# Reordering the front, the attention seam and the layer seam of a two-layer graph-attention kernel

## The chip, the cores and the metric

The kernel runs on one core of one Trainium2 chip. The metric is the device time of one execution in microseconds. All engines of the core (TensorE, VectorE, ScalarE, GpSimd, SyncE) run their own instruction queues in order and meet at semaphores.

## The reference

x has 3327 rows of 256, adj is a 0/1 matrix of 3327 x 3327. Two blocks follow one another, each ahead of a layer norm with relu and with a residual. Cut to what matters:

```
h = relu(layernorm(x))
# block 0: graph attention (both adjacencies are adj)
hs = h @ W_sa ; g = h @ W_gcnb
e = where(adj, exp(-leaky(s_left + s_right)), 0)   # s_left, s_right = hs @ a_sa
x_a = (e @ hs) / (rowsum(e) + 1e-5) ; x_b = adj @ g + b
x = x + sigmoid(gate_a * x_a + gate_b * x_b)        # gates: sigmoid of adj @ h and h against Wa, Wb
# block 1: two layers
y = relu(layernorm(x))
for W in W_stack:                                    # 256 x 512
    Wh, Ws = split(y @ W)
    a = softmax(Wh @ Ws.T) * adj
    y = leaky_relu(a @ Wh + y)
out = x + y
```

## The kernel before, in words

Rows are cut into 26 tiles of 128, 13 pairs of 256 rows (PAIRS) and 13 units of 256 columns (UNITS). Every product is made in three passes of a high and a low part (`product3`, line 1349: 6 matmuls for 256 rows deep), so each operand is evicted from PSUM twice: a high part by ScalarE (ACT) and the remainder, the low part, by VectorE (DVE).

**Front** (the loops `for p in range(PAIRS)`, lines 652, 1033, 1432, and 513 on GpSimd (POOL)). For each pair of tiles: layer norm (`statistics`, `variances`, on POOL the power `inverse_root`, `scales`, `normalise`), a transpose of the pair on TensorE (PE) (`transpose0`), evicted by `transposed_high` and `transposed_low`, the products G (`products_g`, `g_high`, `g_low`) and H (`products_h`, `h2_high`, `h2_low`, which also copies the scores s_right, s_left). From pair 2 on PE takes one unit of block 0's attention (`unit0`, lines 1422 to 1426, 20 matmuls) after each pair; its operand is made by `leaky0`, `exp0` (ACT), `mask0` (DVE), `high0` (ACT), `low0` (DVE). Transposes, G and H share four banks of PSUM in a ring; `turn(pr, i)` numbers the uses (i = 0 the transpose, 1 and 2 G, 3 and 4 H), `projected(i)` waits for the low part of the use four turns before. Before the change the transpose of pair p+1 is at the head of iteration p. Then come 169 units of `unit0` in all, N_LATE says up to which unit leaky, high and exp stand in that order. Adjacency comes by POOL's DMA queue, six stages ahead (`load_unit`).

**Block 1.** Projections `project_wh(n)` (n 0 to 12 layer 1, 13 to 25 layer 2) and `project_q(b)`, then an order written out by hand in steps v. In step v PE makes the scores of unit g (`scores`, S_AT) and weighs the unit 16 steps older (`weigh`, A_AT; after unit CH = 169 four steps more, GAP). Between them a unit goes: `maximum` (DVE), `evict` (ACT, line 706), `subtract` (POOL, 534), `exponent` (ACT, 718), `mask` (DVE, 1158) and `total` (DVE, 1168), `high` (ACT, 752), `low` (POOL, 541), `weigh` (PE, 1562 to 1565). Scores use banks 0 and 1, exponents banks 2 and 3, sums over a block 4 and 5, Q and the turned maximum 6, turned sums 7. A block b is 13 units. At its end of scores (S_END) the maximum is turned (`turn_max`, `row_max`, `spread_max`, `turn_max_back`, `keep_max`); at its end of weighing (A_END) the sum (`turn_sum`, `row_sum`), and the reciprocal comes back in one of two ways: for a block in NEAR by `spread_rec`, `turn_sum_back` and `keep_rec`, for the others by DMA (`store_rec`, `load_rec`, R_END three steps later). Then `weighted`, `residual` twice, `leaky`, `x2_high`, `x2_low`; x2 of blocks 0 to 11 is stored and loaded back by SP (`store_x2`, `load_x2`), block 12's goes straight to XT. The layer's W is split into high and low parts at step v = 154 (lines 872, 1318, 1320).

**Layer seam** (WH_AT): steps 181 to 187 hold projections 13 to 25, with the weighing of layer 1's last units to step LAST1 = 184 and layer 2's scores of block 13 going on. Their banks and waits before the change:

```
334 def wh_bank(n):
338     return 5 if u < 4 else 2 + u % 2
716 if g == CH: act.wait_ge(wh_lo, LAYERS * UNITS)
1507 pe.wait_ge(x2_d, PAIRS - 1); pe.wait_ge(wh_lo, n)          # u < 4
1510 pe.wait_ge(sum_d, CH); pe.wait_ge(wh_lo, n - 1)            # u >= 4
```

The last block (LB = 25) is weighed with rows as outputs (`row_exponent`, line 728, `turn_last`, line 1576, `weigh_last`).

## Time and profile before

| what | value |
|---|---|
| median of 3 runs | 1569.0 us (1568.11 to 1570.0) |
| the profiled execution's own time | 1568.53 us |
| its span | 1566.7 us |
| PE busy | 1533.8 us, 98% |
| DVE, ACT, POOL busy | 1130.7, 1068.2, 983.9 us |
| front with the first attention units | 0 to about 89 us |
| block 0's attention to | about 484 us |
| layer seam | about 1030 to 1070 us |

Times of rows are microseconds from the span's start. A timeline row gives start, busy time, engine, line, operation, output and input, count, and in brackets how long the engine sat idle before it and what ended that. Rows on one engine follow one another a little closer than their busy times, since the end of one overlaps the start of the next. A wait for several semaphores is put down to the one that came last.

### The profile page before, as it was taken

To read this page: it belongs to the slowest core of one execution; us is meant where nothing else is said; L and a number is where in the kernel's file an instruction comes from. 1 tells how busy PE (TensorE), PEld (TensorE's weight loads), DVE (VectorE), ACT (ScalarE), POOL (GpSimd) and SP (SyncE) were. 2 spreads that over 40 slices of the span, in tenths; PEclk is the share of its full clock that TensorE was granted. 3 is DMA by queue.
4 is the path that set the end of the run, shared out by engine and by line. 5 is a ranking of instruction groups with operands and counts; after the bars stand their busy time and mean duration, and the time that the engine had idled before them with its cause. 6 is when DMAs were issued, how large, how long until landed. Compare 5 with 4: busy or idle time off the path is not lost.

```text
span 1566.7 us, 34636 instructions
## 1 busy us (share of the span) xinstructions
PE 1533.8 (98%) x12826; PEld 1524.1 (97%) x12826; DVE 1130.7 (72%) x2119; ACT 1068.2 (68%) x2081; POOL 983.9 (63%) x886
## 2 busy tenths in 40 slices
PE   6999999999999999999999999999999999999998
PEld 5999999999999999999999999999999999999997
DVE  7667666676675677777777777766777777777774
ACT  5689899899984566666666666646666666666666
POOL 4312222222210488888888888847888888888885
PEclk9999999999999999999999999999999999999999
DMA  4354444544440134343433435522443333334343
GB/s 162 65 101 122 116 119 117 149 117 120 116 101 28 42 92 106 107 109 99 107 107 107 111 105 174 183 62 81 104 105 104 104 105 105 104 105 105 105 108 106
DMA packets 98423, 167.83 MB, mean 107 GB/s; under 512 B 15951, under 2 KB 28878, under 8 KB 97998
## 3 DMA queue, kind: packets, MB, share of 16 engines
q1 hardware_dynamic: 70208, 117.75, 27.3%
q0 software_dynamic: 24336, 44.31, 12.0%
q10 hardware_dynamic: 3710, 3.56, 0.7%
q8 instruction: 101, 1.65, 0.5%
q14 instruction: 68, 0.56, 0.1%
HBM read 152.44 MB, written 13.14 MB: 106 GB/s over the span
## 4 chain that ended last, share of the span: by engine, by line
PE 88%; issue 4%; DVE 3%; DMA 2%; POOL 2%; ACT 1%; SPq 0%; DVEq 0%; POOLq 0%; ACTq 0%
PE PS L1349 32%; PE PS L1562 9%; PE PS L1565 9%; PE PS L1564 9%; PE PS L1426 5%; PE PS L1423 5%; PE PS L1425 5%; PE PS L1424 5%; PE PS L1422 5%; POOL FR L541 1%; DMA STGT<-adjt 1%; DMA ROW<-rec_scratch 1%; DMA rec_scratch<-COL 1%; POOL X L534 1%; DVE AF L1158 0%
## 5 line engine op out<-in xcount | busy, mean ns | idle before, releaser
L541 POOL TENSOR_TENSOR FR<-AF,FR 128x512 fp32r<-128x512 f32 x338 | 451.3, 1335 | 124.4 <-ACT FR L752 118.6
L1349 PE MATMUL PS<-FR,RB 128*128 128x256 f32 x3900 | 513.9, 281 | 1.8 <-ACT X L706 1.7
L1349 PEld LDWEIGHTS PS<-FR,RB 128*128 128x128 f32 x3900 | 481.7, 188 | 3.1 <-ACT X L706 3.0
L534 POOL TENSOR_TENSOR X<-X,ROW 128x512 f32<-128x512 f32 x283 | 369.2, 1305 | 81.9 <-ACT ROW L762 81.9
L1562 PE MATMUL PS<-FR,RA 128*128 128x256 f32 x1300 | 370.7, 285 | 3.2 <-POOL FR L541 3.2
L1565 PE MATMUL PS<-FR,RA 128*128 128x256 f32 x1300 | 365.0, 281 | 0.0
L1564 PE MATMUL PS<-FR,RA 128*128 128x256 f32 x1300 | 364.4, 280 | 0.0
L481 POOL DMA_DIRECT2D STGT<-adjt x169 | 91.3, 540 | 298.0 <-PE PS L1426 295.9
L1158 DVE TENSOR_TENSOR AF<-PS,AJ 128x512 f32<-128x512 f32 x338 | 231.1, 684 | 56.1 <-ACT PS L718 46.1
L706 ACT ACTIVATE X<-PS 128x512 f32<-128x512 f32 x272 | 162.5, 597 | 158.8 <-DVE AF L1090 151.4
L1090 DVE TENSOR_TENSOR AF<-PS,AF 128x512 f32<-128x512 f32 x286 | 196.4, 687 | 101.0 <-PE PS L1349 98.6
L1562 PEld LDWEIGHTS PS<-FR,RA 128*128 128x128 f32 x1300 | 244.9, 188 | 5.6 <-POOL FR L541 3.9
L1564 PEld LDWEIGHTS PS<-FR,RA 128*128 128x128 f32 x1300 | 245.1, 189 | 0.0
L1565 PEld LDWEIGHTS PS<-FR,RA 128*128 128x128 f32 x1300 | 244.9, 188 | 0.0
L752 ACT ACTIVATE FR<-AF 128x512 fp32r<-128x512 f32 x338 | 214.0, 633 | 44.6 <-DVE AF L1158 40.4
L718 ACT ACTIVATE PS<-X 128x512 f32<-128x512 f32 x283 | 167.9, 593 | 56.5 <-POOL X L534 54.9
L1168 DVE TENSOR_TENSOR AF<-PS,AF 128x512 f32<-128x512 f32 x300 | 203.8, 679 | 0.0
L1422 PE MATMUL PS<-RA,FR 128*128 128x258 f32 x676 | 191.5, 283 | 3.1 <-DVE FR L967 3.1
L1426 PE MATMUL PS<-RB,STGT 128*128 128x258 f32 x676 | 192.2, 284 | 0.0
L1423 PE MATMUL PS<-RA,FR 128*128 128x256 f32 x676 | 191.5, 283 | 0.0
L1425 PE MATMUL PS<-RB,STGT 128*128 128x258 f32 x676 | 191.3, 283 | 0.0
L1424 PE MATMUL PS<-RA,FR 128*128 128x258 f32 x676 | 190.4, 282 | 0.0
(175 smaller groups left out, 2408.1 us busy)
## 6 DMA issues: line engine op xcount, KB each, us to landing
AJ<-adjt SPq DMA_DIRECT2D x338, 256.0 KB, 2.7
STGT<-adjt POOLq DMA_DIRECT2D x169, 256.0 KB, 3.0
xt_scratch<-ROW SPq DMA_DIRECT2D x12, 512.0 KB, 2.6
RB<-xt_scratch SPq DMA_DIRECT2D x12, 512.0 KB, 5.3
x_scratch<-X ACTq DMA_DIRECT2D x13, 256.0 KB, 2.2
ROW<-x_scratch SPq DMA_DIRECT2D x13, 256.0 KB, 3.2
out<-ROW SPq DMA_DIRECT2D x12, 256.0 KB, 3.4
ROW<-rec_scratch SPq DMA_DIRECT2D x22, 128.0 KB, 3.8
```

Source lines behind the costliest of these rows:

```text
L534: nc.gpsimd.tensor_tensor(slot, slot, MB.unsqueeze(1).broadcast_to([P, 2, 256]), ALU.subtract)\
L541: nc.gpsimd.tensor_tensor(LO[g % 2], WA[g % 2], HI[g % 3].bitcast(F32), ALU.subtract)\
L1158: nc.vector.tensor_tensor(WA[g % 2], PS[:, 2 + g % 2, :], ADJ[g % NADJ], ALU.mult).then_inc(mask_d, 1)
L1349: last = nc.tensor.matmul(out, stationary(a, k), moving(b, k), start=(k == 0 and i == 0), stop=(k == K - 1 and i == 2))
L1422: nc.tensor.matmul(e_to[:, 0:GX], e_hi, RA[:, j, 0:GX], start=first, stop=False)
L1423: nc.tensor.matmul(e_to[:, 0:D], e_hi, RA[:, j, GX:GX + D], start=False, stop=False)
L1424: nc.tensor.matmul(e_to[:, 0:GX], e_lo, RA[:, j, 0:GX], start=False, stop=final)
L1425: nc.tensor.matmul(a_to[:, 0:GX], adj, G[:, j, 0:GX], start=first, stop=False)
L1426: last = nc.tensor.matmul(a_to[:, 0:GX], adj, G[:, j, GX:2 * GX], start=False, stop=final)
L1562: nc.tensor.matmul(to, w_hi_, hi, start=(u == 0 and h == 0 and d == 0), stop=False, skip_group_check=True)
L1564: nc.tensor.matmul(to, w_hi_, lo, start=False, stop=False, skip_group_check=True)
L1565: last = nc.tensor.matmul(to, w_lo_, hi, start=False, stop=final, skip_group_check=True)
```

## The change

In the front the transpose of pair p+1 goes between G and H of pair p, on PE, ACT and DVE, with a new numbering of turns; DVE takes the first low part ahead of the variances, the mask ahead of G's low parts, `scales` of a chain at the end of the same pair; POOL's power goes ahead of the load. In block 1 project_wh(2) goes ahead of project_q(0), xt_low(12) one step later; W's split goes to steps 159 and 160. Block 11 leaves NEAR (reciprocal by DMA) but keeps x2 on chip; block 24's reciprocal comes two steps later. In the layer seam the projections use banks 5, 0, 1, 2, 3, evictions (EV_AT) have steps of their own, block 13's maximum is turned before the scores. The diff, cut:

```
-N_LATE = UNITS + 1
+N_LATE = 2 * UNITS + 1
+EV_AT = dict(WH_AT)
+EV_AT |= {182: (13,), 183: (14,), 184: (15, 16, 17, 18, 19, 20), 185: (21,), 186: (22,), 187: (23, 24), 188: (25,)}
+WH2_BANK = (5, 0, 1, 5, 0, 1, 2, 3, 5, 2, 3, 5, 2)
 WH_AT |= {181: (13,), 182: (14,), 183: (15,), 184: (16, 17, 18, 19, 20, 21), 185: (22,), 186: (23, 24), 187: (25,)}
+W2_AT = 159
-NEAR = (PAIRS - 2, PAIRS - 1, LB - 1)
+NEAR = (PAIRS - 1, LB - 1)
+FAR_X2 = PAIRS - 2
-R_END = {v + 3 * (b not in NEAR): b for v, b in A_END.items()}
+R_END = {v + (0 if b == PAIRS - 1 else 2 if b == LB - 1 else 3): b for v, b in A_END.items()}
...
-            return 5 if u < 4 else 2 + u % 2
+            return WH2_BANK[u]
         def turn(pr, i):
-            return 5 * pr + i + 1 if i else max(5 * pr - 4, 0)
+            return 5 * pr + (0, 1, 2, 4, 5)[i] if i else max(5 * pr - 2, 0)
         def bank_of(pr, i):
-            return 0 if turn(pr, i) == 1 else 4 + turn(pr, i) % 4
+            return 4 + turn(pr, i) % 4
...
@@ SP, load_x1 and steps @@
-                    sp.wait_ge(x2_st, 16 * (PAIRS - 1))
+                    sp.wait_ge(x2_st, 16 * FAR_X2)
...
-                if b is not None and b < PAIRS - 1:
+                if b is not None and b < FAR_X2:
                     store_x2(b)
-                for u in range(PAIRS - 1):
+                for u in range(FAR_X2):
@@ POOL @@
-            normalise(2)
-            for p in range(1, PAIRS - 2):
-                if p - 1 in LN_CHAIN:
-                    i = LN_CHAIN[p - 1]
-                    inverse_root(i, *LN_PARTS[i])
-                normalise(p + 2)
+            for p in range(PAIRS - 2):
+                normalise(p + 2)
+                if p in LN_CHAIN:
+                    i = LN_CHAIN[p]
+                    inverse_root(i, *LN_PARTS[i])
@@ ACT front @@
             for p in range(PAIRS):
-                if 1 <= p < PAIRS - 1:
-                    transposed_high(p + 1)
...
                 g_high(p, 0)
+                if p == PAIRS - 1:
+                    high0(p - 1)
                 g_high(p, 1)
-                if p == 0:
-                    transposed_high(1)
-                if p >= 2:
-                    high0(p - 1)
+                if p < PAIRS - 1:
+                    transposed_high(p + 1)
...
+                if 2 <= p < PAIRS - 1:
+                    high0(p - 1)
                 h2_high(p, 0)
@@ ACT exponent @@
-                if g == CH:
-                    act.wait_ge(wh_lo, LAYERS * UNITS)
+                if CH <= g < CH + 2:
+                    act.wait_ge(wh_lo, UNITS + 1 + max(m for m in range(UNITS) if WH2_BANK[m] == 2 + g % 2))
@@ ACT x2_high @@
-                if b == PAIRS - 1:
+                if b >= FAR_X2:
+                    act.wait_ge(s_mm, CH)
@@ ACT before and in the steps @@
+            wh_high(2)
             q_high(0)
             post_store(PAIRS - 1)
-            wh_high(2)
...
-                if A_END.get(v - 1) in NEAR and v - 1 != LAST1:
-                    keep_rec(A_END[v - 1])
-                if x is not None and x < GL:
+                if x is not None and x < GL and x != CH:
                     exponent(x)
                 if e is not None:
                     evict(e)
+                if x == CH:
+                    exponent(x)
...
+                if A_END.get(v - 2) == LB - 1:
+                    keep_rec(LB - 1)
-                if v == a_step(GL) + 2:
+                if v == a_step(GL) + 3:
                     keep_rows()
...
-                for i, n in enumerate(WH_AT.get(v, ())):
+                for i, n in enumerate(EV_AT.get(v, ())):
+                    if v == LAST1 and i == 1:
+                        spread_rec(A_END[v])
                     wh_high(n)
-                    if v == LAST1 and i == 0:
+                    if v == LAST1 and i == 1:
                         keep_rec(A_END[v])
-                    if v == LAST1 and i == 2:
+                    if v == LAST1 and i == 3:
                         x2_high(A_END[v])
@@ DVE front @@
-            dve.wait_ge(x_in[1], 16)
-            statistics(2, 4)
             dve.wait_ge(wg_hi, 1)
...
             dve.wait_ge(x_in[1], 16)
+            statistics(2, 4)
             statistics(4, 6)
+            transposed_low(0)
             variances(1, 2, 6, 3)
-            transposed_low(0)
             scales(1, 2, 6)
...
             for p in range(PAIRS):
-                if 1 <= p < PAIRS - 1:
-                    transposed_low(p + 1)
-                g_low(p, 0)
-                if p - 1 in LN_CHAIN:
-                    i = LN_CHAIN[p - 1]
-                    scales(i, *LN_PARTS[i])
                 if p >= 2:
                     mask0(p - 1)
+                g_low(p, 0)
                 g_low(p, 1)
-                if p == 0:
-                    transposed_low(1)
+                if p < PAIRS - 1:
+                    transposed_low(p + 1)
...
+                if p in LN_CHAIN:
+                    i = LN_CHAIN[p]
+                    variances(i, *LN_PARTS[i], 3 + sum(b <= LN_PARTS[i][1] for a, b in LN_STATS.values()))
                 if p == 1:
                     mask0(0)
+                if p == PAIRS - 1:
+                    low0(p - 1)
                 h2_low(p, 0)
-                if p >= 1:
+                if 1 <= p < PAIRS - 1:
                     low0(p - 1)
                 h2_low(p, 1)
                 if p in LN_CHAIN:
                     i = LN_CHAIN[p]
-                    variances(i, *LN_PARTS[i], 3 + sum(b <= LN_PARTS[i][1] for a, b in LN_STATS.values()))
+                    scales(i, *LN_PARTS[i])
@@ DVE steps @@
+            wh_low(2)
             q_low(0)
             post_norm(PAIRS - 1)
-            wh_low(2)
...
-                if v == 154:
-                    dve.wait_ge(w_hi, 4)
+                if v == W2_AT:
+                    dve.wait_ge(w_hi, 3)
...
+                if v == W2_AT + 1:
+                    dve.wait_ge(w_hi, 4)
...
-                if v == X12_AT:
+                if v == X12_AT + 1:
                     xt_low(PAIRS - 1)
@@ PE front @@
             for p in range(PAIRS):
-                if 1 <= p < PAIRS - 1:
-                    transpose0(p + 1)
                 pe.wait_ge(htlo_done, p + 1)
                 products_g(p)
-                if p == 0:
-                    transpose0(1)
-                    pe.wait_ge(w_ready, 1)
                 if p == 1:
                     turn_left()
+                if p < PAIRS - 1:
+                    transpose0(p + 1)
+                if p == 0:
+                    pe.wait_ge(w_ready, 1)
                 products_h(p)
@@ PE project_wh @@
-                elif u < 4:
+                elif wh_bank(n) in WH2_BANK[:u]:
+                    pe.wait_ge(wh_lo, UNITS + 1 + max(m for m in range(u) if WH2_BANK[m] == WH2_BANK[u]))
+                else:
                     pe.wait_ge(x2_d, PAIRS - 1)
-                    pe.wait_ge(wh_lo, n)
-                else:
-                    pe.wait_ge(sum_d, CH)
-                    pe.wait_ge(wh_lo, n - 1)
+                    if wh_bank(n) < 2:
+                        pe.wait_ge(ev_d, SEAM)
+                    elif wh_bank(n) < 4:
+                        pe.wait_ge(sum_d, CH)
@@ PE scores @@
+                if SEAM <= g < SEAM + 2:
+                    pe.wait_ge(wh_lo, UNITS + 1 + max(m for m in range(UNITS) if WH2_BANK[m] == g % 2))
...
-                if b == PAIRS and u == UNITS - 1:
-                    pe.wait_ge(x2_d, PAIRS)
+                if b == PAIRS and u >= FAR_X2:
+                    pe.wait_ge(x2_d, u + 1)
@@ PE steps @@
+            project_wh(2)
             project_q(0)
-            for n in range(2, 6):
+            for n in range(3, 6):
...
+                if S_END.get(v - 1) == PAIRS:
+                    turn_max(PAIRS)
                 if s is not None:
                     scores(s)
...
                 for i, n in enumerate(WH_AT.get(v, ())):
+                    if i == 0 and S_END.get(v - 1) == PAIRS:
+                        turn_max_back(PAIRS)
                     project_wh(n)
```

## Rows read from the trace of the kernel before

**Rows 1.** The page, part 4: the chain that ended last, by engine.

```profile
PE 88%; issue 4%; DVE 3%; DMA 2%; POOL 2%; ACT 1%; SPq 0%; DVEq 0%; POOLq 0%; ACTq 0%
```

**Rows 2.** Windows: length, busy us (x instructions) PE, PEld, DVE, ACT, POOL; clock, DMA share, GB/s.

```profile
8.60:35.00 26.40, 20.00 (x141) 19.00 (x142) 21.99 (x80) 16.25 (x41) 13.70 (x18) 1.00 0.44 151
945.00:960.00 15.00, 14.61 (x121) 14.14 (x120) 11.53 (x19) 9.28 (x18) 11.40 (x10) 1.00 0.26 73
999.50:1018.00 18.50, 18.04 (x151) 17.63 (x151) 15.39 (x27) 11.95 (x23) 16.10 (x13) 1.00 0.41 123
1030.60:1070.40 39.80, 35.64 (x286) 34.03 (x286) 22.59 (x39) 17.85 (x34) 11.45 (x10) 1.00 0.11 30
1150.00:1500.00 350.00, 350.00 (x2972) 350.00 (x2971) 267.38 (x455) 214.97 (x383) 297.98 (x232) 1.00 0.39 105
1528.00:1543.00 15.00, 12.54 (x102) 11.55 (x102) 10.86 (x21) 11.45 (x34) 8.83 (x7) 1.00 0.33 93
```

**Rows 3.** Timeline of DVE: start, us, engine, line, form, count [idle before <-releaser].

```profile
8.77 0.68 DVE L1022 TENSOR_TENSOR WX<-AJ,WX 128x516 fp32r<-128x516 f32 x1
...
10.15 0.38 DVE L902 BATCH_NORM_AGGREGATE MV<-ROW 128x2 f32<-128x6 f32 x4
...
11.47 0.68 DVE L934 SCALAR_TENSOR_TENSOR FR<-PS,FR 128x512 fp32r<-128x512 f32 x1
...
13.47 0.79 DVE L928 TENSOR_SCALAR AF<-X,LNT 128x256 f32<-128x256 f32 x2
```

**Rows 4.** Timeline of PE in the front.

```profile
12.29 2.92 PE L1349 MATMUL PS<-WX,FR 128*128 128x258 f32 x12 [3.79 <-DVE FR L934]
15.01 1.06 PE L1376 MATMUL PS<-IDN,AF 128*128 128x128 f32 x4
...
58.34 0.28 PE L1422 MATMUL PS<-RA,FR 128*128 128x258 f32 x1
```

**Rows 5.** Timeline of DVE and ACT over one pair of the front.

```profile
38.40 0.15 DVE L952 COPY XS<-PS 128x4 f32<-128x4 f32 x1
...
39.59 0.63 ACT L596 ACTIVATE AF<-AF 128x512 f32<-128x512 f32 x1
...
40.87 0.68 DVE L961 TENSOR_TENSOR AF<-AF,STGT 128x512 f32<-128x512 f32 x1
...
41.80 1.39 DVE L894 BATCH_NORM_STATS2 ROW<-X 128x6 f32<-128x256 f32 x4
...
44.11 0.15 DVE L952 COPY XS<-PS 128x4 f32<-128x4 f32 x1
```

**Rows 6.** Timeline of PE and DVE at the start of the second attention.

```profile
487.62 1.67 PE L1349 MATMUL PS<-RB,WX 128*128 128x256 f32 x12 [1.28 <-DVE RB L1065]
...
493.34 0.68 DVE L1072 TENSOR_TENSOR RA<-PS,RA 128x512 fp32r<-128x512 f32 x1
...
508.81 1.68 PE L1349 MATMUL PS<-FR,RB 128*128 128x256 f32 x12 [0.61 <-ACT X L706]
```

**Rows 7.** Timeline of DVE, the second subtraction of W.

```profile
949.64 1.78 DVE L1320 TENSOR_TENSOR WX<-ROW,WX 128x512 fp32r<-128x512 f32 x1
```

**Rows 8.** Timeline of DVE, weighting of block 10.

```profile
972.49 0.70 DVE L1197 TENSOR_TENSOR PS<-PS,ROW 128x512 f32<-128x512 f32 x1 [1.71 <-DMA ROW<-rec_scratch]
```

**Rows 9.** Timeline of PE and ACT in the layer seam.

```profile
1037.69 0.39 PE L1562 MATMUL PS<-FR,RA 128*128 128x256 f32 x1 [0.87 <-POOL FR L541]
...
1049.50 3.06 PE L1349 MATMUL PS<-WX,RB 128*128 128x256 f32 x24 [0.28 <-DVE RA L1072]
...
1065.45 0.60 ACT L718 ACTIVATE PS<-X 128x512 f32<-128x512 f32 x1 [0.84 <-DVE RA L1072]
...
1068.96 0.36 PE L1562 MATMUL PS<-FR,RA 128*128 128x256 f32 x1 [0.66 <-POOL FR L541]
```

**Rows 10.** Timeline of DVE and PE in the tail.

```profile
1536.43 0.70 DVE L1197 TENSOR_TENSOR PS<-PS,ROW 128x512 f32<-128x512 f32 x1 [2.46 <-ACT ROW L771]
...
1539.42 0.66 PE L1576 MATMUL PS<-IDN,PEB 128*128 128x128 f32 x4 [1.65 <-ACT PEB L728]
```

More of the change, by code:

```diff
@@ L864, in _ @@
                     spread_max(S_END[v - 1])
-                if A_END.get(v) in NEAR:
+                if A_END.get(v) in NEAR and v != LAST1:
                     spread_rec(A_END[v])
@@ L1356, in projected @@
                     return
-                i -= 8 if i - 4 == turn(PAIRS, 0) else 4
+                i -= 4
                 if i == 0:
@@ L1361, in projected @@
                     q, j = (i - 1) // 5, (i - 1) % 5
-                    if j == 0 and q == 0:
-                        return
-                    if j == 0:
+                    if j == 2:
                         pe.wait_ge(htlo_done, q + 2)
-                    elif j < 3:
-                        pe.wait_ge(glo_done, 2 * q + j)
+                    elif j < 2:
+                        pe.wait_ge(glo_done, 2 * q + j + 1)
                     else:
@@ L1489, in project_q @@
                     pe.wait_ge(wx_ready, 5)
-                if b >= PAIRS and i < PAIRS - 1:
+                if b >= PAIRS and i < FAR_X2:
                     pe.wait_ge(xt2_in[i % 4], 16 * (i // 4 + 1))
@@ L1552, in weigh @@
                 if b == PAIRS:
-                    pe.wait_ge(wh_lo, UNITS + max(4, u + 1))
+                    pe.wait_ge(wh_lo, UNITS + max(1 + max(m for m in range(UNITS) if WH2_BANK[m] == 4 + b % 2), u + 1))
                 pe.wait_ge(alo_d, g + 1)
@@ L1694, in _ @@
                 for i, n in enumerate(WH_AT.get(v, ())):
+                    if i == 0 and S_END.get(v - 1) == PAIRS:
+                        turn_max_back(PAIRS)
                     project_wh(n)
-                    if i == 0 and S_END.get(v - 1) is not None:
+                    if i == 0 and S_END.get(v - 1) not in (None, PAIRS):
                         turn_max_back(S_END[v - 1])
```

17 lines of the change are left out of this document (9 added, 8 removed).

## Prediction

> **What bounds the kernel now.** I read the page first, then the stretches where TensorE (PE) does not keep its pace, then the order of events in each. On the page 88% of the chain that ended last runs over PE [rows 1]. So the time is PE's work plus PE's holes, and the change neither adds nor removes a product of weight: it takes out two small transposes and moves the rest. What is to be had is holes only. The windows show their size [rows 2]. In the undisturbed 1150 to 1500 us, 2972 matmuls take 350 us, 0.118 us each, and nothing is lost; twelve (one unit of scores, one of weighting, one projection) are 1.41 us. At that price 8.6 to 35 us holds 141 matmuls or 16.6 us of work in 26.4 us; 945 to 960 loses 0.7; 999.5 to 1018 loses 0.7; the seam between the two layers (1030.6 to 1070.4) has 286 or 33.7 in 39.8, so 6.1 lost; the tail 1528 to 1543 has 102 or 12.0 in 15, so 3.0 lost. Single waits stand in the timeline. A few matmul records may be missing, so the losses are upper bounds.
>
> **Front, start.** Today the low part of the first transpose stands behind the statistics, the aggregates and the variance adds. It starts at 11.47 [rows 3] and the first products at 12.29 [rows 4]. In the change it takes the place of the aggregates (10.15), and the subtraction at 8.77 moves ahead of the wait on x; so about 9.5, and products at 10.35: 1.9 us earlier. But the second transpose needs normalise(1), at 13.47 on VectorE (DVE), which hangs on the power on GpSimd (POOL) and does not move. Its two operations take 0.79; so the transpose starts at 14.35 instead of 15.01. 0.7 is left, and H waits for the same.
>
> The first twelve products took 2.92 us [rows 4], 0.24 each against 0.118 later, while the granted clock reads 1.00 in the window row. That pace is the lower of the two levels (1.2 GHz), after four transposes and 3.79 us without work. The change leaves a hole of about 1.2 us before the second transpose. Were H and G behind it at the low level too, 24 products would take 2.9 us more. I charge nothing, because the next wait (the turn of the left scores, bound by DVE at 19 to 20 us) covers about half of it and the DVE loop below the rest. The Trainium skill (TensorE: Matmul & The Clock Gate, Part 1: The HAM clock gate) says the half-rate clock follows idleness; by it the new hole would speak against this part.
>
> **Front, per pair.** One pair's loop today: the copy of the right scores (38.40), exp (39.59), mask (40.87), statistics (41.80), next copy (44.11) [rows 5]: 5.7 us. PE has 24 products, 4 transposes and 20 unit matmuls per pair, the same 5.7 us. The transposed low part (0.6) hides today in DVE's wait for G's high part. In the change mask comes first (exp starts 1.19 after the copy, 0.65 more to its end and hand-over: 1.85), then two G low parts (0.34 each), the transposed low part 0.6, statistics 1.31, H low 0.40, unit low 0.60. With the mask's 0.60 that is 6.0 us while statistics last (pairs up to 4), 4.7 after. And the new order of PSUM turns makes H(p,1) wait for G's low part of the same pair, behind that mask; T(p+1) now waits for H's low part of the pair before. Walking pair by pair with today's start-to-start times I find the gain of the start gone by pair 2, whose unit products begin 0.8 late, those of pair 4 0.9 late, and those of pair 7 at 58.8 against 58.34 [rows 4]: **0.5 lost**. After pair 5 the low part of G is ready 1.3 us after G begins and H(p,1) asks for it at 2.5 less the hand-over, 2.1: it holds, 5.7 again. Bounds: 3 gained (the start's 1.9 and two of today's waits) to 4 lost. The power goes ahead of one load of adjacency on POOL's queue, 1.7 us later for a stage wanted six units on: nothing. The stall near 101 us on a load behind the strided store of scores keeps its place, both issue in the same order. N_LATE only keeps leaky, high, exp in the old order for 13 more units, 2.0 us of ScalarE (ACT) work per unit of 2.4: nothing.
>
> **Start of the second attention.** PE waits 1.28 us for the last transposed low part before project_q(0) [rows 6]; project_wh(2) now stands there. But project_wh(5) needs wh_low(3), which stays behind post_scales at 493.34; so it starts at about 493.8 instead of 494.1 and most of the hoist becomes a later hole. With one refill less, **0.4** (0 to 1.3). The wait of 0.61 at 508.81 exists because xt_low(12) stands ahead of maximum(6); it moves behind it: **0.7** with the refill (0.3 to 0.8).
>
> **W of layer two.** Two subtractions with both inputs in SBUF sit in one step; the second takes 1.78 us and ends at 951.4 [rows 7], right before the turn of a block's maximum, for which PE waits: the 0.7 lost in that window. They go to steps 159 and 160. There DVE has 1.0 us free per step (three operations of 0.6 in 2.82), but block 10's residual work (five of 0.6) follows from step 162. **0.4** (0.6 lost to 0.9 gained).
>
> **Block 11 by DMA.** The two transposes back go (128 columns each, about 0.06, and a refill), and x2's store and load; the reciprocal goes by store and broadcast, three steps later. Today PE loses 0.7 there [rows 2] besides; the far block 10 loses too, its weighting waits 1.71 us for that DMA [rows 8]. **0.3** (1.0 lost to 1.2 gained). SP's queue gets a small store and a 128 KB broadcast ahead of one adjacency load, and loses 1 MB.
>
> **Layer seam.** Today a projection's high and low parts stand in the same step ahead of the next exponent: PE waits 0.87 at 1037.69. Projections share bank 5 or two banks, so each waits for a forerunner's low part (0.28 and a refill at 1049.50). Then come block 13's maximum and an eviction, and weigh(169) waits 0.66 for low(169) at 1068.96, because exponent(169), at 1065.45, waits for all 26 low parts [rows 9]. With five banks no projection waits: each bank's last reader is two or more projections back, 2.8 us, against 1.3 for high and low. Evictions are a step late, so exponents 167 and 168 go first; turn_max goes before the scores and its back turn before wh(23). By hand: wh(13..15) at 1032.1, 1034.9, 1037.8; wh(16..21) 1040.9 to 1049.8 (block 12's x2 done at 1048.5, in time for scores(181)); scores(184) end at 1061.8; exponent(169) starts at 1060.4 and takes 3.5 us through mask, high and POOL's low, as today from 1065.45 to 1068.96, so weigh(169) starts at 1063.9 after a hole of 0.7. exponent(170) waits for wh_low(25): 0.3 more. So 5.1 less 0.3, **4.8** (2 to 6.1).
>
> **Tail.** Block 24's reciprocal comes two steps later. Today DVE's weighted(24) waits 2.46 us, to 1536.43, ahead of a mask; its high part and an exponent follow, for whose transpose PE waits 1.65 us [rows 10]. Moved, mask(326) needs only its own transpose; the wait goes. weighted(24) then delays mask(328), 0.2 back. **1.5** (0 to 2.1).
>
> **Sum.** -0.5 + 0.4 + 0.7 + 0.4 + 0.3 + 4.8 + 1.5 = 7.6 us off the profiled execution's 1568.5: 1560.9. The median of the runs is 1569.0, 0.5 above it; I forecast 1561.2 us for it. A measurement of this kernel can tell about 0.2% (3.1 us) from no change.
>
> **Rivals.** (1) The front is worth more: if ACT and DVE run ahead where I have them wait, the start's 1.9 lives: 2.5 us less, 1558.7. For: PE has 9.8 us of holes before 35. Against: the 6.0 us loop. 0.15. (2) The seam gives half: exponents 169 and 170 still wait for low parts of projections 23 and 25 behind ACT's queue; 2.4 in place of 4.8, with the tail at 0.5: 1564.6. For: the 3.5 us chain behind the exponent is untouched. 0.14. (3) DVE and POOL shut each other out: both moved subtractions take 1.78, not one, and block 10's work queues behind them, 1.0 us of stall: W's term -0.6, 1562.2. For: one already took 1.78 while POOL, 85% busy in steady state (297.98 of 350 us), ran. 0.10. The skill's page SBUF — State Buffer (Who interferes with whom) states it as a rule: such a DVE operation and a GpSimd operation block one another for a whole instruction; the trace agrees. (4) Slower: H(p,1)'s new wait on G's low part binds in every pair after 5 too. It decides once the low part comes over 2.1 us after G begins, where I find 1.3; the whole is slower only if ten pairs lose over 0.8 us each. At 1.4 each, 14 less the 8.1 of the other terms is 6 on top: 1575. For: all of DVE's front work is now in that chain. 0.04. (5) The holes reappear behind POOL's 2.6 us per step, and nothing that can be measured is left: 1567 to 1569. 0.05.
>
> **From this to the numbers.** The main case has 0.52, with 1558.5 to 1564. Case 1 reaches 1557, case 2 1566. The range of 1557 to 1566.5 leaves out cases 4 and 5 and the edges of the others. Faster by over 0.2% means under 1565.9: the main case, cases 1 and 3 and three quarters of case 2, 0.87. Same 0.09, slower 0.04.
>
> **What would show it.** First products at about 10.3 us, unit products of pair 7 at 58.3 to 59.3. No PE wait before project_q(0), one near 493; none on ACT at 508. From projection 13 to weigh(169) 31.8 us where today has 36.9, with no wait on a projection's low part before scores(184). The 1.65 us of the tail gone. I am wrong if PE's holes before 89 us shrink or grow by over 2, or if the seam gives under 3.

## The result, and the profile after

The kernel after takes **1559.0 us** (median of 4 runs, 1557.3 to 1559.3) against 1568.55 us for the kernel before on the same chip (4 runs, 1568.0 to 1570.0): a ratio of 0.9941, 95% interval 0.9929 to 0.9953. That is 9.6 us faster. The forecast was 1561.2 us, from 1557 to 1566.5. The profiled execution took 1559.26 us with a span of 1557.5 us, so 9.3 us less than the profiled one of before.

The page first. The chain that ended last now runs over PE for 91% where it was 88% [rows 1]; the work on PE is the same, so what went is holes:

```profile
PE 91%; issue 2%; DVE 2%; DMA 2%; POOL 1%; ACT 1%; POOLq 0%; SPq 0%; DVEq 0%; ACTq 0%
```

Then the same stretches as in [rows 2], each moved to where that work now lies (columns as there: length, busy us and instructions of PE, PEld, DVE, ACT and POOL, clock, DMA share, GB/s):

```profile
8.60:35.00 26.40, 20.34 (x128) 19.08 (x128) 21.29 (x82) 15.99 (x42) 14.19 (x20) 1.00 0.44 148
942.50:957.50 15.00, 15.00 (x130) 15.00 (x129) 10.28 (x19) 9.58 (x18) 12.13 (x11) 1.00 0.27 74
998.10:1015.40 17.30, 17.30 (x151) 17.30 (x150) 14.61 (x25) 10.87 (x19) 16.05 (x13) 1.00 0.48 105
1028.00:1062.80 34.80, 34.31 (x291) 34.13 (x290) 22.49 (x39) 17.49 (x34) 11.21 (x10) 1.00 0.11 31
1150.00:1500.00 350.00, 350.00 (x2973) 350.00 (x2972) 266.66 (x453) 216.10 (x384) 298.66 (x232) 1.00 0.41 105
1520.30:1535.30 15.00, 13.99 (x115) 13.03 (x114) 10.81 (x21) 12.01 (x36) 9.05 (x7) 1.00 0.37 107
```

Three things stand out. The two windows around layer two's W and block 11 are full, 15.00 of 15 and 17.30 of 17.3 us. The seam's work fills 34.31 of 34.8 us, where 35.64 of 39.8 was busy before. And the front has not gained: 128 matmuls in 26.4 us where 141 were before, in the same stretch; its holes are as large as ever. The steady stretch is the same to one instruction (2973 and 2972), so nothing comes from there.

**Where the 9.3 us lie.** I laid the two timelines of PE over one another by their order of instructions and read after minus before at the same instruction: -0.1 at the first full unit of the front (unit 15, 102 us); +0.2 at 496; -0.4 at 510; -0.4 at 700; -1.5 at 800; -2.4 at 960; -1.3 at 982; -2.6 at 1015; -7.6 at 1065; -7.7 at 1520; -9.2 at 1553. The code between 541 and 940 us is the same in both kernels, so the 1.1 us between 700 and 800 belongs to those two executions and not to the change (the traces of e7, e8, e9 and e10, with that same code, have steps of 0.3 to 0.7 us there too), and so may other steps of that size. That is why each part was then undone by itself.

The rows that answer to the forecast's. PE in the front and at the start of the second attention (timeline: start, us, engine, line, form, count, idle before and its releaser), for [rows 4] and [rows 6]:

```profile
10.36 2.92 PE L1361 MATMUL PS<-WX,FR 128*128 128x258 f32 x12 [1.89 <-DVE FR L945]
13.92 1.11 PE L1386 MATMUL PS<-IDN,AF 128*128 128x128 f32 x4 [0.64 <-DVE AF L939]
14.69 5.25 PE L1361 MATMUL PS<-WX,FR 128*128 128x260 f32 x24
...
28.10 0.99 PE L1361 MATMUL PS<-WX,FR 128*128 128x260 f32 x6 [1.41 <-DVE RB L953]
...
59.47 0.28 PE L1432 MATMUL PS<-RA,FR 128*128 128x258 f32 x1
...
102.39 0.39 PE L1432 MATMUL PS<-RA,FR 128*128 128x258 f32 x1 [1.28 <-DVE FR L978]
...
494.40 1.65 PE L1361 MATMUL PS<-WX,RB 128*128 128x256 f32 x12 [2.03 <-DVE RA L1082]
```

The first products start at 10.36, as forecast (10.35). At 14.69, 24 products take 5.25 us, 0.22 each: by their pace still the lower level (1.2 GHz) that the first twelve had, although the column of the granted clock reads 1.00 there. At 28.10 is the new wait of H(2,1) for the low part of its own pair's G. Pair 7's unit products start at 59.47, 1.13 us later than before. The wait ahead of project_q(0) is gone and one of 2.03 stands ahead of project_wh(5).

DVE around block 10's residual work, for [rows 7] and [rows 8]:

```profile
962.33 1.74 DVE L1328 TENSOR_TENSOR WX<-ROW,WX 128x512 fp32r<-128x512 f32 x1 [0.62 <-ACT WX L880]
966.49 1.37 DVE L1332 TENSOR_TENSOR WX<-ROW,WX 128x512 fp32r<-128x512 f32 x1 [0.62 <-ACT WX L882]
971.20 0.70 DVE L1207 TENSOR_TENSOR PS<-PS,ROW 128x512 f32<-128x512 f32 x1 [0.95 <-DMA ROW<-rec_scratch]
```

PE in the seam, for [rows 9]:

```profile
1039.80 7.37 PE L1361 MATMUL PS<-WX,RB 128*128 128x256 f32 x60
...
1060.87 0.35 PE L1576 MATMUL PS<-FR,RA 128*128 128x256 f32 x1 [0.49 <-POOL FR L546]
...
1064.20 0.36 PE L1576 MATMUL PS<-FR,RA 128*128 128x256 f32 x1 [0.28 <-POOL FR L546]
```

Five projections run in one piece, and from projection 13 (1029.49) to weigh(169) (1060.87) it is 31.38 us: 36.90 before, 31.8 forecast.

### The profile page after: what moved, and what is told of

Its sections match the earlier page's. It is cut to its first block, busy times and chain, and to the rows that moved or that the text cites. A ratio compares the mean times of both kernels' runs of the same rounds, so it can differ in the third digit from the quotient of the medians.

```text
span 1557.5 us, 34619 instructions
## 1 busy us (share of the span) xinstructions
PE 1531.8 (98%) x12824; PEld 1524.5 (98%) x12824; DVE 1132.0 (73%) x2119; ACT 1068.5 (69%) x2079; POOL 982.1 (63%) x886
## 3 DMA queue, kind: packets, MB, share of 16 engines
q8 instruction: 101, 1.65, 0.5%
## 4 chain that ended last, share of the span: by engine, by line
PE 91%; issue 2%; DVE 2%; DMA 2%; POOL 1%; ACT 1%; POOLq 0%; SPq 0%; DVEq 0%; ACTq 0%
PE PS L1361 34%; PE PS L1576 9%; PE PS L1579 9%; PE PS L1578 9%; PE PS L1436 5%; PE PS L1433 5%; PE PS L1435 5%; PE PS L1432 5%; PE PS L1434 5%; POOL FR L546 1%; DMA STGT<-adjt 1%; DMA ROW<-rec_scratch 0%; POOL X L539 0%; DMA X<-xt 0%; DVE ROW L905 0%
## 5 line engine op out<-in xcount | busy, mean ns | idle before, releaser
L972 DVE TENSOR_TENSOR AF<-AF,STGT 128x512 f32<-128x512 f32 x169 | 116.8, 691 | 111.3 <-ACT AF L601 100.0
L1432 PE MATMUL PS<-RA,FR 128*128 128x258 f32 x676 | 191.6, 283 | 2.3 <-DVE FR L978 2.2
```

The source lines that it names most:

```text
L1432: nc.tensor.matmul(e_to[:, 0:GX], e_hi, RA[:, j, 0:GX], start=first, stop=False)
```

## The experiments

Each is the kernel after with one edit (e7: two, e12: three); the edits are shown cut. A profile's place can be read to 0.1 us, but two executions of one code differ by about 1 us, so with each result stands what its trace shows at the place of the edit. Ratios are to the kernel before on the same chip; several of these chips ran all kernels 0.5 to 3 us slower or faster than the first.

**e1, the seam.**

```
-WH2_BANK = (5, 0, 1, 5, 0, 1, 2, 3, 5, 2, 3, 5, 2)
+return 5 if u < 4 else 2 + u % 2
-EV_AT |= {182: (13,), 183: (14,), 184: (15, ..., 20), ...}
+EV_AT = WH_AT
+(turn of maximum behind the scores)
```

> The kernel after, with the seam of the kernel before alone: all projections of layer two in bank 5 or in banks 2 and 3, their high and low parts in their own step, the turn of block 13's maximum behind the scores. My theory (the seam's order is the term of 4.8 us, and the two profiles put 5.0 there): 1559.0 + 5.0 = 1564.0 us; from projection 13 to weigh(169) 36.5 to 37 us in place of 31.4; the waits 0.87 at exponent 168's place and 0.66 ahead of weigh(169) are back. Rival (the seam gains half only, and the rest of the fall behind projection 13 is block 11's x2 that needs no store and load any more): 1561.5, from projection 13 to weigh(169) 34 us. Rival (the profiles differ by chance elsewhere and the seam is worth all of the fall): over 1565.

Measured: 1564.16 us (10 runs), ratio 0.9976 (0.9967 to 0.9985). The three other kernels of that chip keep the new seam: 1558.23 (e2), 1559.28 (e3) and 1560.30 us (e4). PE:

```profile
1028.75 1.60 PE L1353 MATMUL PS<-WX,RB 128*128 128x256 f32 x12
...
1065.63 0.36 PE L1563 MATMUL PS<-FR,RA 128*128 128x256 f32 x1 [0.65 <-POOL FR L542]
```

36.88 us, with the old waits. Against after it loses 5.5 us up to weigh(169), and 4.97 us once weigh(170) is through, since after waits 0.28 there and a little behind. The seam's order is worth 5.0, forecast 4.8. My theory stands, both rivals fall.

**e11, the turn of the maximum alone.**

```
-if S_END.get(v - 1) == PAIRS: turn_max(PAIRS)      (ahead of the scores)
+if S_END.get(v - 1) is not None: turn_max(...)      (behind them; the back turn behind project_wh)
```

> The kernel after, with only the turn of block 13's maximum back behind the scores and behind the first projection of its step; banks and evictions of the seam as in after. Theory A (the banks carry the seam's gain, the turn's place little): 0 to 0.7 us slower, 1559.0 to 1559.7, from projection 13 to weigh(169) 31.4 to 32.1. Rival B (the kernel with the whole old seam waited 0.84 us for that maximum's turn and 1.14 us for an eviction behind it, and both belong to the turn's place): 2.0 us slower, 33.4.

Measured: 1559.97 us, ratio 0.9933 (0.9918 to 0.9947). 31.90 us from projection 13 to weigh(169), whose wait grows from 0.49 to 0.99; 0.5 there and 0.2 behind. Theory A: banks and eviction times carry 4.3, the turn's place 0.7.

**e2, the front as before; e3, the old pair loop with the new start and the new last pair.**

> The kernel after, with the front of the kernel before alone (transposes ahead of the products of G, turns, low part of the first transpose behind the variances, power behind, last pair's unit products in their old place). The two profiles: the products of G of the last pair start 1.07 us later in after, unit 15 of the front 0.09 us earlier. Theory A (the loss of the pairs is given back at the last pair and at the wait for a load of adjacency near 101 us): first products at 12.3 in place of 10.36 us, G of the last pair at 83.8, unit 15 at 102.4 to 102.6, time 1559.1, within 0.4 of after. Rival B (my forecast's term, 0.5 lost, is still there at the end): 1558.5. Rival C (the start's 1.9 us lives on in part): 1560 or more.

> The kernel after, with the pair loop and the turns of the kernel before, but the new start (low part of the first transpose ahead of the variances) and the new place of the unit's parts in the last pair. Theory A (what sets the end of the front is the load of adjacency behind the strided store of the scores, near 101 us): first products at 10.4, G of the last pair at 83.6 to 84.0, and yet unit 15 at 102.2 to 102.5 with a wait of 2 us or more ahead of it; time 1558.6 to 1559.2. Rival B (the new pair loop costs its 1.07 us to the end): unit 15 at 101.3, time 1557.9. Rival C (the start's gain is not eaten up by the old loop either): unit 15 at 100.5 or before, 1557.0.

Measured: e2 1558.23 us, ratio 0.9943 (0.9928 to 0.9958); e3 1559.28 us, 0.9947 (0.9930 to 0.9963). Neither can be told from after. The traces tell why, for e3 (first DVE, then PE):

```profile
101.58 0.69 DVE L977 TENSOR_TENSOR AF<-AF,STGT 128x512 f32<-128x512 f32 x1 [4.09 <-DMA STGT<-adjt]
...
93.82 0.36 PE L1441 MATMUL PS<-RA,FR 128*128 128x258 f32 x1 [2.40 <-DVE FR L983]
102.93 0.39 PE L1441 MATMUL PS<-RA,FR 128*128 128x258 f32 x1 [0.19 <-DVE FR L983]
```

In e3 the last pair's products of G start 1.6 us before those of after (83.25 and 84.84), and two things take that back. The first is the chain on ACT and DVE behind the last pair. Its start, the copy of the last right scores on DVE, did not move with PE (DVE, first of after, then of e3):

```profile
88.34 0.23 DVE L963 COPY XS<-PS 128x4 f32<-128x4 f32 x2 [0.21 <-ACT RA L581]
88.56 0.22 DVE L968 COPY XS<-PS 128x4 f32<-128x4 f32 x2
```

In before it stands at 88.40 and in e2 at 88.51. Leaky, exp, mask, high and low part of unit 12 hang on it, so unit 12 starts at 93.62 in after, 93.67 in before, 93.78 in e2 and 93.82 in e3, whose wait there is 2.40 us in place of 0.94. What the old loops had gained on PE is gone at this place. Behind its wait of 2.40 us e3 then ran 3.4 us at a granted clock of 0.50 and was 1.7 us behind after at 100 us.

The second is the load of adjacency. It is issued by POOL when PE has done unit 10, so earlier in e3, and yet lands later. The store of the left scores, which SP issues behind that same copy, decides (POOL's issue and SP's, first of after, then of e3):

```profile
88.60 0.37 SPq L375 DMA_DIRECT2D sl_scratch<-XS  x1
90.58 0.53 POOL L488 DMA_DIRECT2D STGT<-adjt  x1 [4.75 <-PE PS L1436]
...
88.81 0.37 SPq L376 DMA_DIRECT2D sl_scratch<-XS  x1
89.01 0.53 POOL L489 DMA_DIRECT2D STGT<-adjt  x1 [4.76 <-PE PS L1445]
```

The mask of unit 16 waits for this load until 101.04 in after, 101.14 in before, 101.58 in e3 and 102.04 in e2. The low part of unit 15 stands behind that mask on DVE, and PE waits for it. (No run puts that low part first. Its high part was done at 97.4 us in after, so an estimate from these rows is that most of PE's 1.28 us at 102.39 would go: unit 16 could follow at about 103.1, two units' work from 98.4 on end at 103.3.) This wait took up 1.1 of the 1.7 us by which e3 was late. So theory A holds for the time, and the load is only the second half of its reason: a lead of PE of up to 2.2 us in the pairs (e3 at 50 us) is gone at unit 12. e2's profiled execution was 2.3 to 2.8 us slower than its others. Against after it loses 0.8 us by the later load (PE waits 2.13 us) and 1.5 in 3.4 us at a granted clock of 0.50 behind it.

What the traces also show, and none of the expectations had: time that the copy of the scores gains does live on. The 24 products at 14.69 took 5.25 us in after, but 3.15 to 3.75 in e4, e9, e11 and e12, whose front is the same code (PE of e4):

```profile
14.35 3.15 PE L1363 MATMUL PS<-WX,FR 128*128 128x260 f32 x24
```

With a start 0.2 to 0.3 us earlier and these faster products e4, e9 and e11 have everything 0.8 to 0.9 us before after from 40 to 100 us, the copy of the scores and the store too. In e4 the load then lands 0.7 us earlier, and 0.7 are left at 110 us; in e11 the store takes 0.5 us longer and 0.1 is left.

**e4, block 11.**

```
-NEAR = (PAIRS - 1, LB - 1)
-FAR_X2 = PAIRS - 2
+NEAR = (PAIRS - 2, PAIRS - 1, LB - 1)
+FAR_X2 = PAIRS - 1
+(R_END and keep_rec of block 11 as before)
```

> The kernel after, with block 11 as in the kernel before alone: its reciprocal turned back over PE at once, its residual work three steps earlier, its x2 stored and loaded again. The two profiles put 1.2 us of gain between step 171 and 177 (1002 to 1018 us), where I had forecast 0.3. Theory A (that gain is this change's): from weigh's step at 1002 to the step at 1015 to 1018 1.2 us longer, a DVE or POOL wait of PE back there, 1560.2. Rival B (0.3 as forecast, the rest lies between two executions of one code): 1559.3. Rival C (with block 11's work moved away, the waits of block 10's stage get shorter instead): no change, 1558.8 to 1559.1.

Measured: 1560.30 us, ratio 0.9953 (0.9938 to 0.9968). From the same instruction at 1001 to that at 1015 us it takes 1.33 us more than after; before took 1.31 more. PE waits 0.31 for POOL's low part at 1011.82 again, as before did at 1013.65. By instruction 0.6 of the 1.33 us lie at that weighing, 0.4 at the one before it and 0.2 at the two transposes back. Theory A; the forecast's 0.3 was too small by 1.0.

**e5, W in step 154; e6, W in steps 143 and 153.**

```
e5: -if v == W2_AT: ...          e6: -W2_AT = 159
    -if v == W2_AT + 1: ...          +W2_AT = 153
    +if v == 154: (both)             +the part WX[..., 0:D] in step W2_AT - 10
```

> The kernel after, with both subtractions of layer two's W and their two copies back in step 154. Theory A (one of the subtractions at 1.78 us stood right ahead of the turn of block 11's maximum, and now it doesn't; what the moved ones cost later is small): 0.9 us lost again between 945 and 957 us, 0.1 to 0.2 got back at block 10's residual work up to 982, 0.8 net, 1559.8 us. My forecast's term was 0.4: 1559.4. Rival (both subtractions slow, block 10's work late by 1.0, net -0.6 for the change): 1558.4.

> The kernel after, with the first of the two subtractions (the part of W that no step after 15 reads) in step 143 and the other in step 153, in place of steps 159 and 160. Theory A (a subtraction costs PE nothing where no block's residual work and no turn follows within two steps; the wait of 0.32 us for POOL's low part near 971 us is the queue that they leave behind): no PE wait between 930 and 970 us, the 0.32 gone, 0.3 us less, 1558.7. Rival (it is block 10's own work that makes that wait): as after, 1559.0. Rival (one at 1.78 us in step 153 is already too late for the turn of block 11's maximum at step 156): 0.3 to 0.8 us more.

Measured: e5 1562.28 us, ratio 0.9951 (0.9936 to 0.9966); e6 1561.64 us, 0.9946 (0.9931 to 0.9961). Between 940 and 982 us e5 loses 0.33 us against after's profile, e6 gains 1.29, but e1, e3, e7 and e8, whose W is as in after, gain 1.01 to 1.05 too. After's own profiled execution had a late landing of block 10's reciprocal there, the 0.95 of DVE shown above: weighted(10) starts 1.0 us later than in e1 to e4 and e7 to e11, which have no such wait. Against those nine e5 loses 1.4 and e6 gains 0.25; the kernel before loses 0.8. The trace of e5:

```profile
949.56 0.86 DVE L1327 TENSOR_TENSOR WX<-ROW,WX 128x512 fp32r<-128x512 f32 x1 [1.14 <-ACT WX L881]
950.35 1.78 DVE L1329 TENSOR_TENSOR WX<-ROW,WX 128x512 fp32r<-128x512 f32 x1
...
973.71 0.70 DVE L1206 TENSOR_TENSOR PS<-PS,ROW 128x512 f32<-128x512 f32 x1 [2.21 <-DMA ROW<-rec_scratch]
```

The slow subtraction is back, and 0.97 us are lost by 960 us (0.94 in before). Behind it before wins 0.1 back and e5 loses 0.4 more, as that landing falls: in e5 it is 0.5 us later on the common time than in before. So the move of W is worth 0.8 to 1.4 us, theory A. e12, with e6's edit, gains 0.7 against the nine where e6 gains 0.25, so a few tenths here are chance. The moved subtractions took 1.74 and 1.37 us, as rival 3 of the forecast had it, yet in the nine without a late reciprocal they cost PE no more than one wait of 0.31 to 0.32 us, near 971 in after's time, and that one is gone in e6, which has one of 0.19 at 979 instead.

**e7, tail and start of the second attention.**

```
-R_END ... 2 if b == LB - 1      -wh_low(2); q_low(0); ...
+R_END ... 0 if b == LB - 1      +q_low(0); ...; wh_low(2)
                                 -if v == X12_AT + 1:   +if v == X12_AT:
```

> The kernel after, with two far apart parts as in the kernel before: block 24's reciprocal kept and used two steps earlier (the tail), and at the start of the second attention projection 2 behind project_q(0) and the last transposed low part ahead of a maximum. My theory, part by part: the tail 1.5 us slower, with a wait of PE of 1.6 us for the row turn near 1531 us (rival: the gain of the tail comes from something ahead of it, under 0.5); the order of the projections 0.0 (a wait of 1.3 ahead of project_q(0) back, the one of 2.0 ahead of project_wh(5) gone; my forecast said 0.4); the transposed low part 0.6 slower, with PE's wait of 0.6 near 508 us back (rival: 0). Together 1561.1 us; rival 1559.3.

Measured: 1563.38 us, ratio 0.9954 (0.9938 to 0.9971). PE's timeline:

```profile
490.39 1.66 PE L1361 MATMUL PS<-RB,WX 128*128 128x256 f32 x12 [1.28 <-DVE RB L1075]
...
495.36 1.92 PE L1361 MATMUL PS<-WX,RB 128*128 128x256 f32 x13 [0.48 <-DVE RA L1082]
...
511.54 1.68 PE L1361 MATMUL PS<-FR,RB 128*128 128x256 f32 x12 [0.61 <-ACT X L711]
...
1534.43 0.66 PE L1590 MATMUL PS<-IDN,PEB 128*128 128x128 f32 x4 [1.67 <-ACT PEB L733]
```

By place: 1.5 us more in the tail, 0.00 at 496 us (waits of 1.28 and 0.48 in place of one of 2.03), 0.57 at 510. All three as my theory had it.

**e10, projection 3's low part earlier.**

```
 post_norm(PAIRS - 1)
+wh_low(3)
 post_scales(PAIRS - 1)
-wh_low(3)
```

> The kernel after, with the low part of projection 3 ahead of the last pair's scales on DVE (its high part has been there since 491.6 us, the low part starts at 493.6 today). Theory A (the hoist of projection 2 gained nothing because project_wh(5) then waits for this low part behind the scales): the wait of 2.03 us at 494.4 goes, scores(0) at 493.9 to 494.2 in place of 495.9, 1.7 to 2.0 us less: 1557.1. Rival B (scores(0) or the first maximum waits for something of the same age, the query's low part or the last transposed one): under 0.7 gained. Rival C (the first units of the second attention are bound by DVE, which has the same work to do, and the time is back by step 6): 0.

Measured: **1558.46 us, ratio 0.9920 (0.9903 to 0.9936)**, on a chip where before took 1571.31; the fastest against before of all. Its trace, first PE, then DVE:

```profile
494.17 1.66 PE L1361 MATMUL PS<-WX,RB 128*128 128x256 f32 x12 [0.45 <-DVE RA L1082]
495.66 1.59 PE L1361 MATMUL PS<-FR,RB 128*128 128x256 f32 x12
...
493.34 0.68 DVE L1082 TENSOR_TENSOR RA<-PS,RA 128x512 fp32r<-128x512 f32 x1
494.24 0.16 DVE L923 TENSOR_TENSOR LNT<-LNT 128x2 f32<-128x2 f32 x1 [0.22 <-POOL LNT L493]
```

1.54 us less at its place: the wait of 2.03 falls to 0.45. This execution is 1.3 us late from the front, so the starts are to be read against one another: the low part at 493.34 here would be at 492.0 in after's time, where it was at 493.56. Theory A in the main, 1.54 where 1.7 to 2.0 were expected; 0.45 remains, and the norm's statistics and aggregates (492.13 to 493.3) still stand ahead of the low part. Its ratio's interval overlaps that of after (0.9929 to 0.9953), so the 1.5 us rest on the trace at this place. e12, which has the same edit, gains the same 1.54 there. No run moves this low part without the hoist of projection 2, so it is not shown that the two need one another.

**e8, e9, e12, the store of the left scores.** The load behind which the front ends is issued at 90.6 us, just behind a store of 1536 elements of 4 bytes (88.6).

```
e8:  SL_PARTS = [(1, 7), (7, PAIRS - 1), (PAIRS - 1, PAIRS)]
e9:  if i: sp.wait_ge(lr_done, 20)
e12: e8's parts; if i == 2: sp.wait_ge(lr_done, 32); e10's and e6's edits
```

> The kernel after, with the second store of the left scores (pairs 7 to 12, 1536 elements of 4 bytes, issued at 88.6 us) cut in two: pairs 7 to 11 at about 83.7 and pair 12 at 88.6 or later. Theory A (that store holds up the load of adjacency issued at 90.6 until 101, and PE's 1.28 us at unit 15 is that): the load lands before 98, DVE's wait of 3.75 us at 101 and PE's 1.28 go, unit 15 at 101.1 to 101.4, 1557.9. Rival B (the earlier store now holds up the load issued at 85.3 just as long): a DVE wait on adjacency near 96 to 97, no gain or up to 1 us lost. Rival C (the load-back of the scores, which comes later behind three stores than behind two, is what the second block waits for): up to 1.5 us more after 102.

> The kernel after, with the second store of the left scores (and the load that brings them back) held until 20 units of the first attention have had their leaky step, near 112 us, in place of 88.6; block 7, at some 280 us, is the first that reads them. In the profiles so far the load of adjacency issued at 90.6 landed at 101.0 to 102.5, and behind the longer of these waits TensorE ran 2.5 to 3.5 us at the lower level of its clock. Theory A (the store is what holds that load): it lands before 96, no DVE wait for adjacency near 101, unit 15 at 101.1, no lower clock at 103 to 107; the store at 112 delays one load by 8 to 11 us, against five units of 2.4 us that it has, so 0 to 1.5 us lost there. 1557.0 us on the chip of the profile of after, and 1.3 to 4 us less than the other variants on one chip. Rival B (any place of the store costs the same stall, now near 122 us, for five units are no more than 12 us): as after. Rival C (the load waits for something else at that time): the stall stays at 101 us.

> Three edits on the kernel after: (1) low part of projection 3 ahead of the last pair's scales, as in e10; (2) the two subtractions of layer two's W in steps 143 and 153, as in e6; (3) the second store of the left scores cut in two, pairs 7 to 11 at about 83.6 us and pair 12, 256 elements, held until 32 units have had their leaky step, near 130 us, where nothing is queued with it but the adjacency. Theory A (the store of 4-byte elements holds the loads of adjacency for a time that goes with its number of elements): the load issued at 85 lands by 97, unit 15 at 101.3 or before, and the 256 elements at 130 are stored in 2 to 4 us without a wait of PE; 1.2 us less there than after's profile, 1.6 less at the start of the second attention, 0.3 at W: ratio to before 0.990 to 0.991. Rival B (any such store takes its 10 to 12 us, whatever its size, as the 256 elements behind the load-back did in e8 with 10.7): a stall of PE of 2 to 5 us near 140 us and half a clock behind it: 0.993 to 0.995. Rival C (as e8's slower executions: the load-back of 640 KB at 96 us is what holds the loads, and the stall comes at 103 to 110 us).

Measured: e8 1560.42 us, ratio 0.9938 (0.9920 to 0.9956), its four runs two and two, 1557.6 and 1558.5, 1562.3 and 1563.1. Its profiled execution is one of the two longer ones: DVE waits 0.86 us for adjacency at 97.17, and then, behind the store of the last 256 elements (issued at 96.73, done at 107.46 beside the 768 KB load-back), 5.21 us at 109.62. Rival B has its wait; the longer one stood in no expectation. e9 1564.39 us, 0.9961 (0.9946 to 0.9976). e12 1562.69 us, 0.9947 (0.9934 to 0.9961). In e9 the store went out at 102.70, sooner than the 112 it was meant for. The stall at 101 us is gone, unit 15 starts at 100.06, and DVE waits 7.22 us for adjacency at 115.86 instead, PE 4.95 us. The store took 10.8 us, as elsewhere. The expected 1557.0, with at most 1.5 us lost at the new place, was wrong: there a load is asked for every 2.4 us, and the place is a worse one. e12 shows the store bare (SP's issues, then DVE's wait, then PE's):

```profile
132.86 0.37 SPq L378 DMA_DIRECT2D sl_scratch<-XS  x1
142.19 0.32 SPq L381 DMA_DIRECT2D ROW<-sl_scratch  x1
...
145.04 0.69 DVE L975 TENSOR_TENSOR AF<-AF,STGT 128x512 f32<-128x512 f32 x1 [8.28 <-DMA STGT<-adjt]
...
146.39 0.38 PE L1435 MATMUL PS<-RA,FR 128*128 128x258 f32 x1 [3.87 <-DVE FR L981]
```

256 elements, 1 KB, take 9.3 us, in which the loads all but stand still (windows of PE, with DMA share and GB/s last):

```profile
120.00:132.00 12.00, 12.00 (x102) 1.00 0.52 133
133.00:142.00 9.00, 9.00 (x77) 1.00 0.62 31
```

So the first half of my theory is right, the loads are slow while the store is under way; the second, that the time goes with the number of elements, is wrong, and rival B took its place. The packets say the same. In after all 1552 small packets of the store's queue are recorded before 91.5 us and none between 91.5 and 99.8, when the store is done; in e12 all 272 before 134. What is long is the time behind them. The store at 55 us has no stall behind it; there the pairs ask for a load only every 5.3 to 5.7 us, which is likely why, but no run tests it. What in the chip makes the store long is open: no run changed its queue or its form.

## Why the prediction was right, and where it was not

Its 1561.2 us were 2.2 above what came (its own sum gives 1561.4: 1560.9 and 0.5), the range and the main case held, and the sum's 7.6 us stand against 9.3 in the profiles. By its terms:

| term | forecast | undone alone | from |
|---|---|---|---|
| front | -0.5 | 0 | e2, e3 |
| order of projection 2 | 0.4 | 0.0 | e7 |
| transposed low part 12 | 0.7 | 0.6 | e7 |
| W of layer two | 0.4 | 0.8 (to 1.4) | e5, and before |
| block 11 by DMA | 0.3 | 1.3 | e4 |
| seam | 4.8 | 5.0 | e1 |
| tail | 1.5 | 1.5 | e7 |

The terms undone add up to 9.2, and the profiles differ by 9.3. Among the profiles' steps after's late reciprocal (1.0 lost) and before's 1.1 between 700 and 800 us cancel. That the forecast came this near is in part luck: the front, W, block 11 and the seam were too small by 2.1 together, the two terms of the second attention too large by 0.5.

**Right in mechanism and size** were the seam, the tail and the transposed low part. The seam's hand walk gave the hole ahead of weigh(169) as 0.7 and it was 0.49, wait at weigh(170) 0.3 and 0.28. The tail's 1.65 us went as said, and small waits of 0.16 to 0.46 remained.

**The step that failed in the front** is what was done with the walk's end. The walk said that pair 7 would be 0.46 late; it was 1.13 late (59.47, beyond the 58.3 to 59.3 given as the sign), and the last pair's G 1.07. The late waits were in the places named (the turn's wait for G's low part 1.41 us in pair 2). But I carried a loss of 0.5 to the end, and took PE's lateness in the pairs for the stage's. What goes on from the front is the copy of the last scores on DVE and what hangs on it, unit 12 and the store, and that copy stood at 88.3 to 88.6 us with either loop. The 1.07 us were down to nothing at unit 12 (93.62 against 93.67), ahead of the load.

**The clock in the front** was put at nothing, and in part wrongly. The 24 products at 0.22 each were real in after's execution, and the turn of the left scores covered about half, as said: it starts at 19.78 in after and at 18.73 in e4, whose 24 products took 3.15 us. The DVE loop did not cover the rest, as the 0.8 us that e4, e9 and e11 keep to 100 us show; some 0.2 to 0.3 of them are an earlier start. The forecast also lacked that the new wait of 1.40 us in pair 2 can be followed by a second stretch at the lower level: granted clock 0.50 for 3.4 us from 27 or 28 us on in e4, e5, e6, e7, e10 and e12, not in after, e1, e8, e9 and e11, and not in before, e2 and e3, which have the old loop. It has cost PE about 1.5 us when it is over, and all but 0.2 to 0.3 are back by 40. In the start itself the power and normalise(1), which I had left where they were, came 0.4 us earlier (13.09 for 13.47).

**The hoist of projection 2**: the wait was foreseen at the right instruction, but priced too low: it was 2.03 us, project_wh(5) started at 494.40 and not at 493.8, and the hoist's gain was gone. The last low part stands behind the same scales in both orders, and PE reaches scores(0) when it is done, no sooner (e7: 0.00 at 496 us).

**W** was mis-sized: 0.4 for 0.8 or more. I let block 10's residual work eat up half of the gain. The bound "0.9 gained" was the better reading: the row of 1.78 us ahead of the turn told the price. The rows of rival 3 came true in their first half: the moved subtractions took 1.74 and 1.37 us against 0.86 for the first one in e5. The time did not follow: that rival's term was -0.6, and before and e5 show at least +0.8, since DVE had the room for the surplus. The rule that bears on it stands in the Trainium skill (SBUF — State Buffer, Who interferes with whom): a DVE instruction with two SBUF inputs contends with a GpSimd instruction that reads SBUF. The trace agrees. The subtraction of 962.33 starts 0.1 us after an operation of POOL and ends 0.55 us after it, and POOL's next one takes 1.78 us where others take 1.30:

```profile
962.22 1.30 POOL L546 TENSOR_TENSOR FR<-AF,FR 128x512 fp32r<-128x512 f32 x1
963.47 1.78 POOL L539 TENSOR_TENSOR X<-X,ROW 128x512 f32<-128x512 f32 x1
```

**Block 11** was mis-sized by 1.0. Its window in [rows 2] had 0.7 us of hole beside two turns and a refill, and I set 0.3 because the far block 10 loses too. But block 10's loss is its own: a wait for a DMA [rows 8], small waits of PE for POOL, and in after the two subtractions. Block 11, made far, has a full window (17.30 of 17.3). I took one far block's loss for another's.

Rivals 1, 2, 4 and 5 did not come. Rival 4 has its wait in pairs 2 and 3 only.

## What to carry to other kernels

Before a gain or loss of one engine is carried to the end of a stage, look for the next wait and ask what sets it. If it is another engine's chain or a transfer that the edit does not move, the wait takes up what was gained or lost; here the copy of the last scores on DVE, and the store behind it, set two such waits. A hoist on one engine is worth what the last low part behind it allows (here moving that one too gave 1.5 us for one line). And where single executions differ by 1 us, undo the parts one by one and read each at its own place in the trace, not in the total.

## What the runs showed of the hardware

The store of 4-byte elements from SBUF takes 9.3 us for 256 elements (10.7 beside a large load) and 10.8 to 13.0 for 1280 or 1536, from its issue to that of the load that waits for it. Other loads crawl meanwhile: 21 GB/s in after from 89.5 to 99.5 us and 31 in e12 from 133 to 142, where the kernel otherwise moves 133.

TensorE can fall to its lower level (1.2 GHz) behind a wait, and the length of the wait alone does not decide. The granted clock went to 0.50 behind single waits of 1.75, 2.13, 2.27, 2.40, 2.49, 2.68 and 3.87 us, and within one of 4.95; it did not behind waits of 2.01, 2.36 and 2.91. Behind the wait of 1.40 us in pair 2, with two of 0.7 us shortly ahead of it, it fell in six of eleven executions, and behind the one of 2.02 to 2.04 us at the start of the second attention in two (e4, e9) of ten. Each time but in the longest wait it stayed at 0.50 for 3.4 us; of that, e2, e3, e4's second, e6 and e7 lost 1.2 to 1.5 us each. The load that lands between 100.3 and 102.5 us and this clock are two causes by which the profiled executions differ; for executions without a profile nothing is shown.

```profile
103.00:104.00 1.00, 0.16 (x1) 0.63 1.07 322
104.00:105.00 1.00, 1.00 (x5) 0.50 0.88 299
105.00:106.00 1.00, 1.00 (x7) 0.50 0.96 371
106.00:107.00 1.00, 1.00 (x8) 0.67 0.74 258
107.00:108.00 1.00, 1.00 (x11) 1.00 0.17 59
```

These are windows of PE in e6, around its wait of 2.68 us before 103.84 (length, busy us and matmuls of PE, granted clock, DMA share, GB/s): 5 to 7 matmuls in a microsecond at the lower level, 11 at the higher; the windows at 0.63 and 0.67 hold both levels.
